# Queries and keys of one graph formed node by node and then transposed, the residual's transpose stored whole and split in the expert stage, in a fused graph-attention and mixture-of-experts kernel

## The reference

```python
# attention part, added to x
h = layernorm(x)
q, k, v = h @ Wq.T, h @ Wk.T, h @ Wv.T + bv            # in 12 heads of 32
a = einsum('bnhd,bmhd->bhnm', q, k) * SCALE + adj[:, None]
a = where(all(a == 0, axis=-1), -inf, a)
o = einsum('bhnm,bmhd->bnhd', nan_to_num(softmax(a)), v)
x = x + o @ Wo.T + bo
# expert part, added to x
u = layernorm(x)
logits = mean_over_nodes(u) @ router_w.T + router_b    # the two best experts of each graph
hid = act_e(u @ w1[e] + b1[e])                         # gelu, silu, mish, gelu
y = u + sum_e gate[e] * (hid @ w2[e] + b2[e])
out = x + layernorm(y) * ln_g + ln_b
```

## Time and profile before

| | |
|---|---|
| median of 3 runs | 1639.47 us (1636.82 to 1640.29) |
| the profiled execution, its own time | 1638.12 us |
| its span from first to last instruction | 1636.0 us |
| PE busy | 1590.5 us, 97% of the span |
| DVE busy | 1209.8 us, 74% |
| ACT busy | 955.6 us, 58% |
| POOL busy | 689.6 us, 42% |
| mean granted clock of TensorE | 0.993 of full speed |
| attention stage, first to last `scores` | 25.53 to 699.37 us |

### The profile page before, as it was taken

One profiled execution on the slowest core, in us unless ns is written; L12 is line 12 of the kernel. 1 busy time (PEld: TensorE's weight loads), 2 busy tenths in 40 slices (PEclk: granted clock), 3 DMA queues, 4 the chain that ended last, 5 costly groups with the idle time before them and its releaser, 6 DMA issues.

```text
span 1636.0 us, 46011 instructions
## 1 busy us (share of the span) xinstructions
PE 1590.5 (97%) x12720; PEld 1528.0 (93%) x12721; DVE 1209.8 (74%) x3750; ACT 955.6 (58%) x2819; POOL 689.6 (42%) x1106
## 2 busy tenths in 40 slices
PE   8999999999999999779999999999999999999998
PEld 7999999999999999769999999999999999999998
DVE  5788888888888888657766666676776767677766
ACT  6899999999999988753422232333334323243332
POOL 3787888878888777531111111111111111111112
PEclk9999999999999999889999999999999999999999
DMA  6444433455545543673222222222222222222211
GB/s 190 153 138 138 136 129 132 147 168 182 176 169 172 182 134 133 253 301 105 71 74 74 74 74 74 74 74 74 67 70 71 65 74 74 74 74 65 83 59 45
DMA packets 93804, 189.09 MB, mean 116 GB/s; under 512 B 10337, under 2 KB 57441, under 8 KB 92385
## 3 DMA queue, kind: packets, MB, share of 16 engines
q1 hardware_dynamic: 91664, 170.17, 31.6%
q10 hardware_dynamic: 1872, 15.73, 2.5%
HBM read 108.80 MB, written 77.07 MB: 114 GB/s over the span
## 4 chain that ended last, share of the span: by engine, by line
PE 89%; DVE 3%; issue 2%; ACT 2%; DMA 1%; POOL 1%; DVEq 1%; ACTq 0%; POOLq 0%; SPq 0%
PE bank L460 69%; PE bank L534 5%; PE bank L667 5%; PE bank L487 3%; PE bank L557 3%; PE bank L574 2%; PE bank L543 1%; PE bank L566 1%; DMA ut_scratch<-ut_out 1%; DVE half_t L1371 1%; DVE inverse L1378 1%; DVE inverse L1374 1%; ACT at_hi L944 0%; ACT inverse L951 0%; ACT prob L737 0%
## 5 line engine op out<-in xcount | busy, mean ns | idle before, releaser
L460 PE MATMUL bank<-w_hi,ut_in 128*128 x1536 | 423.7, 343 | 0.8 <-issue 0.4
L460 PE MATMUL bank<-w_both,at_hi 128*128 x1524 | 389.1, 336 | 7.4 <-DVE at_lo L1343 7.3
L737 ACT ACTIVATE prob<-att,heads 128x128 f32<-128x128 f32 x768 | 297.4, 390 | 14.2 <-DVE heads L1108 10.3
L460 PEld LDWEIGHTS bank<-w_both,at_hi 128*128 128x128 f32 x1524 | 274.3, 188 | 12.3 <-issue 12.2
L460 PEld LDWEIGHTS bank<-w_hi,ut_in 128*128 128x128 f32 x1536 | 281.5, 189 | 1.3 <-issue 1.3
L460 PE MATMUL bank<-w_lo,ut_in 128*128 x768 | 258.2, 336 | 0.0
L460 PE MATMUL bank<-w_both,at_lo 128*128 x762 | 255.3, 335 | 0.0
L875 ACT ACTIVATE hid<-hid 128x384 f32<-128x384 f32 x192 | 95.1, 526 | 270.5 <-DVE hid L1264 270.5
L944 ACT ACTIVATE at_hi<-bank,gate_col 128x384 fp32r<-128x384 f32 x254 | 133.4, 576 | 199.6 <-PE bank L667 197.8
L1264 DVE TENSOR_TENSOR hid<-bank,b_wide 128x384 f32<-128x384 f32 x256 | 130.9, 552 | 147.6 <-PE bank L460 138.9
L1072 POOL TENSOR_SCALAR rs_z<-mv_z 128x1 f32<-128x1 f32 x64 | 34.9, 545 | 433.1 <-DVE mv_z L1397 433.1
(11 more groups left out here) (139 smaller groups left out, 3475.7 us busy)
## 6 DMA issues: line engine op xcount, KB each, us to landing
xu_scratch<-xu SPq DMA_DIRECT2D x64, 384.0 KB, 2.3
ut_scratch<-ut_out SPq DMA_DIRECT2D x64, 384.0 KB, 2.7
ut_in<-ut_scratch SPq DMA_DIRECT2D x64, 384.0 KB, 3.0
xz<-xu_scratch SPq DMA_DIRECT2D x64, 384.0 KB, 3.2
x_in<-in_x SPq DMA_DIRECT2D x32, 384.0 KB, 4.7
xu<-in_x SPq DMA_DIRECT2D x32, 384.0 KB, 4.3
out_dram<-xz SPq DMA_DIRECT2D x64, 192.0 KB, 2.2
w_lo<-in_L_ffn_w SPq DMA_DIRECT2D x4, 1152.0 KB, 5.9
```

What stands on the lines that cost most here:

```text
L460: last = nc.tensor.matmul(acc, lhs[c][a], rhs[c][b], start=start and n == 0, stop=stop and n == len(terms) - 1)
L737: nc.scalar.activation(prob[g][:, hh, :], att[g][:, head, :], ACT.Exp, bias=neg_max[g][:, head:head + 1], scale=-1.0, accum_out=row_sum[g] ...
```

## The change

Queries and keys are now formed as values are: the transposed input of one graph is held still and the 384 columns of the weights stream past, which gives nodes on the partitions. Two products of 9 matmuls of 384 columns (`project_qk(h + 1)`) go into one double bank, `both`. DVE copies both to `qk_nat` in one instruction of 768 columns (`take_qk`), PE transposes them in six transposes (`transpose_qk`), and ACT copies and scales them into `q_t` and `k_t`. Each buffer now holds one graph, and the pipeline reaches less far ahead: `transpose_x` works on graph `h + 3` instead of `h + 5`, `project_v` on `h + 1` instead of `h + 2`, and the stage has two steps fewer ahead of step 0.

The transpose of `u` is stored once, unrounded (`take_u`), which removes `rest_of_u` on DVE; the expert stage splits it after it is loaded, with `round_ut` on ACT and `rest_of_ut` on DVE, and `first_layer` waits for the second of these.

On PE `project_v` now stands ahead of `spread_inverse`. On POOL `add_output_bias` works on graph `h - 2` instead of `h - 1` and stands ahead of `root2` instead of behind `fold_scores`. `load_residual` is issued at odd steps. Memory is laid out anew, and the loads of the experts' weights near the end of the stage start at other steps.

```diff
-        STEPS = range(-6, B + 4)
+        STEPS = range(-4, B + 4)
...
-                if h % 2 == 1 and 2 <= t + 4 < PAIRS:
-                    reached(sp, xn_done, 2 * (t + 2) + 2)
-                    load_x(t + 4)
+                if h % 2 == 1 and 2 <= t + 3 < PAIRS:
+                    reached(sp, xn_done, 2 * (t + 1) + 2)
+                    load_x(t + 3)
+                if h % 2 == 1 and 2 <= t < PAIRS:
+                    for g in range(2):
+                        sp.wait_ge(xu_stored[t % 2][g], 16 * (t // 2))
+                    load_residual(t)
...
+                reached(pe, qk_done, 2 * (n + 1))
...
-            def project_qk(h):
-
-                m, t = h % 2, pair(h + 2)
-                if h < 0:
-                    pe.wait_ge(wt_lo_done, (m + 1) * DC)
-                reached(pe, xt_lo_done, 2 * t + 2)
-                reached(pe, qk_done, qk_count(h - 1))
-                reached(pe, ot_done, h - 1)
-                reached(pe, inv_taken, h - 1)
-                for oc in range(DC):
-                    acc = bank[4 + oc // 2][:, (oc % 2) * 2 * N:(oc % 2 + 1) * 2 * N]
-                    last = split_product(acc, [(wt_hi[m][:, c, oc * P:(oc + 1) * P], wt_lo[m][:, c, oc * P:(oc + 1) * P]) for c in range(DC)],
-                                         [(xt_hi[t % 2][:, c, :], xt_lo[t % 2][:, c, :]) for c in range(DC)])
-                    if oc > 0:
-                        last.then_inc(qk_mm, 1)
+            def project_qk(n):
+
+                if n == 0:
+                    pe.wait_ge(wt_lo_done, 2 * DC)
+                reached(pe, xt_lo_done, n + 1)
+                reached(pe, ot_done, n - 2)
+                reached(pe, inv_taken, n - 2)
+                for m in range(2):
+                    last = split_product(both[:, m, 0:D], [(xt_hi[n % 2][:, c, :], xt_lo[n % 2][:, c, :]) for c in range(DC)],
+                                         [(wt_hi[m][:, c, :], wt_lo[m][:, c, :]) for c in range(DC)])
+                last.then_inc(qk_mm, 1)
+
+            def transpose_qk(n):
+                reached(pe, qk_taken, n + 1)
+                for m in range(2):
+                    for c in range(DC):
+                        last = nc.tensor.transpose(both[:, m, c * N:(c + 1) * N], qk_nat[:, m, c * P:(c + 1) * P], ident[:])
+                    last.then_inc(qkt_mm, 1)
...
+                reached(pe, ut_split, b + 1)
...
-                if has_qk(h):
-                    project_qk(h)
+                if has(h + 1):
+                    project_qk(h + 1)
+                if h == -1:
+                    transpose_weights(3)
...
+                if has(h + 1):
+                    transpose_qk(h + 1)
                 if has(h - 3):
                     transpose_u(h - 3)
                 if has(h - 1) and h != B:
                     transpose_probs(h - 1, 2)
+                if has(h + 1):
+                    project_v(h + 1)
                 if has(h - 1):
                     spread_inverse(h - 1)
-                if has(h + 2):
-                    project_v(h + 2)
                 if h == B - 11:
                     logits(0)
                 if has(h - 1):
                     attend(h - 1)
-                if has(h + 5):
-                    transpose_x(h + 5)
-                if h == -4:
-                    transpose_weights(1)
-                    transpose_weights(2)
-                if h == -2:
-                    transpose_weights(3)
+                if has(h + 3):
+                    transpose_x(h + 3)
+                if h in (-3, -2):
+                    transpose_weights(h + 4)
...
+            def take_qk(n):
+                reached(act, s_mm, n)
+                for m, (to, scale) in enumerate(((q_t, SCALE), (k_t, 1.0))):
+                    reached(act, qkt_mm, 2 * n + m + 1)
+                    nc.scalar.activation(flat(to[:]), both[:, m, 0:D], ACT.Copy, scale=scale).then_inc(qk_done, 1)
...
+            def take_u(n):
                 g = n % 2
                 reached(act, ut_mm, n + 1)
                 reached(act, ut_stored[g], 16 * (n // 2))
-                nc.scalar.activation(flat(ut_out[g][:, 0]), bank[3][:, 0:D], ACT.Copy).then_inc(ut_hi_done, 1)
+                nc.scalar.activation(flat(ut_out[g][:]), bank[3][:, 0:D], ACT.Copy).then_inc(ut_taken, 1)
...
+            def load_under_stages(h):
+                e = h - (FIRST + 2 * PIECES + 3)
+                if e == 0:
                     for p in range(3):
                         act.wait_ge(hi_stored[p], 16 * (2 * PIECES // 3))
                         act.wait_ge(lo_stored[p], 16 * (PIECES // 3))
-                    load_w1_hi(0)
-                if h == B - 4:
+                if 0 <= e < E - 1:
+                    load_w1_hi(e)
+                if h == B - 3:
                     act.wait_ge(xn_done, B)
-                    act.wait_ge(v_mm, B - 2)
-                    act.wait_ge(qk_mm, 2 * B - 2)
-                    act.dma_start(b1_wide[:].rearrange("p e s f -> p (e s f)"), b1.rearrange("(o e) f -> o (e f)", o=1).partition_broadcast(P)).then_inc(b1_loaded, 16)
-                    load_w1_hi(1)
-                if h == B - 3:
-                    act.wait_ge(qk_mm, 2 * B)
-                    load_w1_hi(2)
-                    act.wait_ge(s_mm, B - 2)
-                    load_w2("unused", "qk0")
-
-            def load_under_values():
+                    load_w1_hi(E - 1)
+
+            def load_under_projections():
                 act.wait_ge(v_mm, B)
-                load_w1_hi(3)
-                load_w2("xt1", "xt1")
+                load_w2("unused", "wv")
...
+            def round_ut(b, m, lap):
+
+                reached(act, ut_loaded[m % 2], 16 * (2 * lap + m // 2 + 1))
+                nc.scalar.activation(flat(ut_in[m % 2][:, 0]), flat(ut_in[m % 2][:, 1]).bitcast(F32), ACT.Copy).then_inc(ut_rounded, 1)
...
                 if has(h - 1):
                     take_probs(h - 1, 0)
                     take_probs(h - 1, 1)
+                if has(h + 1):
+                    take_qk(h + 1)
                 if h == B - 1:
                     load_under_scores()
-                if h == B:
-                    load_under_probs()
+                if h in (B - 1, B):
+                    load_under_probs(h - 1)
+                if h == B - 1:
+                    round_ut(0, 0, 0)
+                if h == B + 1:
+                    round_ut(1, 1, 0)
                 if has(h - 3):
-                    round_u(h - 3)
+                    take_u(h - 3)
                 if has(h - 1):
                     take_inverse(h - 1)
-                if has(h + 5):
-                    normalise_x(h + 5)
-                if h == -5:
+                if has(h + 3):
+                    normalise_x(h + 3)
...
+                if h == 2:
+                    pool.wait_ge(small_loaded, 16 * (2 + DC))
+                if has(h - 2):
+                    add_output_bias(h - 2)
                 if has(h - 3):
                     root2(h - 3)
                 if has(h):
                     fold_scores(h)
-                if h == 0:
-                    pool.wait_ge(small_loaded, 16 * (2 + DC))
-                if has(h - 1):
-                    add_output_bias(h - 1)
-                if has(h + 6):
-                    root1(h + 6)
+                if has(h + 4):
+                    root1(h + 4)
...
+            def take_qk(n):
+
+                reached(dve, qk_mm, n + 1)
+                reached(dve, qkt_mm, 2 * n)
+                nc.vector.tensor_copy(qk_nat[:], both[:, :, 0:D]).then_inc(qk_taken, 1)
...
-            def rest_of_u(n):
-                g = n % 2
-                reached(dve, ut_hi_done, n + 1)
-                nc.vector.tensor_tensor(flat(ut_out[g][:, 1]), bank[3][:, 0:D], flat(ut_out[g][:, 0]).bitcast(F32), ALU.subtract).then_inc(ut_lo_done, 1)
...
+            def rest_of_ut(b, m, lap):
+                reached(dve, ut_rounded, b + 1)
+                raw_half = flat(ut_in[m % 2][:, 1])
+                nc.vector.tensor_tensor(raw_half, raw_half.bitcast(F32), flat(ut_in[m % 2][:, 0]).bitcast(F32), ALU.subtract).then_inc(ut_split, 1)
...
+                if has(h + 1):
+                    take_qk(h + 1)
...
-                if has(h - 3):
-                    rest_of_u(h - 3)
-                if has(h + 6):
-                    input_stats(h + 6)
-                if h == -2:
+                if h in (B, B + 1):
+                    rest_of_ut(h - B, h - B, 0)
+                if has(h + 4):
+                    input_stats(h + 4)
...
+                if has(h + 1):
+                    take_v(h + 1)
...
+                    if k == 0 and graph(b, 1) and not (isinstance(b, int) and b < 1):
+                        rest_of_ut(b + 1, (m + 1) % 4, lap + (m + 1) // 4)```

The first place is on PE, in the second half of a step in the middle of the attention stage, from the transposes of the probabilities to the transpose of the next normalised input. Before:

```order
```

(31 more changed lines are left out.)

144 lines of the change are left out of this document (51 added, 93 removed).

## The result

The changed kernel takes **1697.8 us** (median of 4 runs, 1693.7 to 1698.9) against 1639.7 of the kernel before (1636.8 to 1640.3): the ratio is 1.035, 95% interval 1.033 to 1.038, so 58 us slower. The forecast was 1702, in a range of 1672 to 1718.

The account below looks back on a forecast made before the run. All four engines were read as close to full, PE busiest; two hand-over loops above PE's 11.25 us were to set a step of 11.78. Terms 59 + 1 + 3 = +63 us gave 1701, stated as 1702, range 1672 to 1718.

Parts of the forecast that it names:

- PE's own work, 11.25 us: Attention step on PE: 10.70 less 0.10 for the matmuls plus 0.65 for six new transposes gives 11.25 us.
- PE's work alone sets the step: Rival for the attention step: both loops shorter than read by 0.5 us, step 11.25, total 1670; chance 0.10.
- The first loop, 11.78: Attention step, take_inverse through POOL's bias and root, normalise_x1, transposes, values and inverse transposes: 11.78 us, setting the step.
- the 1.10 for the bias between guard and root: POOL in the attention step: output bias of 1.03 us and a gap add 1.10 us ahead of root2.
- The second loop, 11.72: Attention step, inverse's transposes, take_inverse, normalising and transposing the next input: 11.72 us, PE standing 0.45 us a step.
- DVE's copy at no cost: Attention step: the 768-column copy takes 0.95 us on DVE, ends before its transposes are due, costs PE nothing.
- The start: Ahead of first scores 2 to 3 us gained, 2 given back after: third scores at 40.8 instead of 41.82.
- The steps: Third to last scores: 61 steps of 11.78 us less 1.0, last scores at 758.4 against 699.37, +59.0 us.
- Behind the last scores: After the last scores: bias ahead of root2 costs 1 us once, expert-stage subtraction 3 us (bounds 0 and 8).
- The stall gone: End of attention stage: POOL's 9.57 us and PE's 8.55 vanish, the last xu load issued earlier, ahead of large weight loads.
- The sum: Whole kernel: 59 + 1 + 3 = +63 us, on the profiled 1638.12 giving 1701, stated as 1702.

Follow-up runs that it names:

- two kernels: Changed kernel with normalise_x ahead of take_inverse and four of six query/key transposes left out: 1658.6 us; the same with the output bias behind root2: 1639.3 us.
- the one on `xn`: Changed kernel with normalise_x(h + 3) moved ahead of take_inverse(h - 1) on ACT: 1669.1 us, ratio 1.018.
- the part alone: Kernel before with only u's transpose stored whole by ACT, then rounded and subtracted in the expert stage: 1639.8 us, ratio 1.000.
- The first experiment on it: Kernel before with only the output bias moved, for graph h - 2 ahead of root2 on POOL: 1638.7 us, ratio 0.999.
- the first experiment: Changed kernel with the output bias on POOL put back behind the folds, for graph h - 1: 1695.3 us, ratio 1.034.

## Why the prediction was right, and where its terms were off

- **PE's own work, 11.25 us.** Measured 11.24, with PE free of waits. The six transposes at 0.109 us were right (0.65 in the trace, 0.64 to 0.66 by doubling them). The 18 matmuls of queries and keys take 304.50 - 301.24 = 3.26 us where 3.23 was forecast and the 27 before took 3.33, and the values 1.66 (309.93 - 308.27) for 1.70. The rival "PE's work alone sets the step" gave 1670; the kernel in which it holds takes 1669.1.
- **The first loop, 11.78.** The loop exists, and two kernels show it by what the bias's place costs. Its size was over-read: `normalise_x1` starts 8.00 us after the last `take_inverse` (306.75 - 298.75, which is 310.45 less one step) and not 8.12. The term at fault is the 1.10 for the bias between guard and root. From its start to the root's it does take 1.10, but it starts 0.17 us after the start of the guard, where the root before started 0.29 us after it (311.96 - 311.67), so only 0.98 is added. With this and the values' 1.66 the loop is about 11.63. The trace agrees that it had slack: ACT ends `xu` at 307.46 and PE comes to it at 307.58, 0.12 us later, where a hand-over takes 0.05.
- **The second loop, 11.72.** Measured 11.70, and PE's stand 0.46 for 0.45. It set the step, by about 0.07 us over the other. So the mechanism was named (two closed loops above PE's work), but the wrong one of the two as the longer; that this cost so little is luck, since they happen to lie close together. The experiment on the bias and the one on `xn` tell them apart.
- **DVE's copy at no cost.** 0.95 us, as sized, over 1.28 us early; a wait for `qk_nat` shows only at the start (1.05 us ahead of 30.41), as said there.
- **The start.** Forecast: third scores at 40.8. Measured 43.30. I had counted 2 to 3 us won ahead of the first scores; it was 0.44. PE waits 1.24 us there for the split of the weights, and the eleven slow matmuls shown above cost about 1.7 us more than at the later pace, which the prediction did not have. This term was off by 2.5 us.
- **The steps.** 61 steps from the third to the last scores took 712.0 us, 11.67 each, against 717.6 in the forecast. With the late start the last scores came at 755.3 for 758.4.
- **Behind the last scores.** +2.6 us for +4. The bias ahead of the root, the expert stage's subtraction and the new order of the weight loads are in it, not told apart; the part alone shows the subtraction as 0.8 us of wait more than the earlier trace rows and nothing that the median can tell. By the Trainium skill's rule a DVE instruction with two SBUF inputs and a GpSimd one that reads SBUF shut each other out (SBUF — State Buffer, section SBUF: two separate sides). The changed kernel's subtractions last 0.545 to 0.561 us each, and no cost of such a lock shows on the path, which does not test the rule.
- **The stall gone.** Right, and for the reason given, the load's place. The first experiment on it tried the bias instead and missed. In the changed kernel the last load of `xu` is issued at 754.21, 0.95 us ahead of 3584 KB of weights (755.16), and a load of `ut_in` at 755.45 just behind them. The order was tested by experiment only on the kernel before, but the times to landing of these two (last column) fit it:

```profile
xu<-in_x SPq DMA_DIRECT2D x1, 384.0 KB, 4.8
...
ut_in<-ut_scratch SPq DMA_DIRECT2D x1, 192.0 KB, 14.3
```


The sum came to 1701 for the profiled execution; it took 1696.8. The 4 us are 5.6 of shorter steps and 1.4 behind them, less 2.5 of start; the rest is rounding in the terms. So the sum is closer than its terms, because the late start and the shorter steps cancel in part.

What stays open: why the first matmuls at the start ran at the slower pace, and whether 2.5 us for the bias in the first experiment is real behind the last scores, as it did not come again.

## What to carry to other kernels

When all engines are busy for three quarters of the time or more, write the step as closed loops of hand-overs, each from one use of a result to the same use a step later, and compare their lengths with the busiest engine's work; moving one instruction past a wait on the same engine (here two rows on ACT) was worth 29 us, half of the whole loss. Loops nest: a place that is worth 2 us under a longer loop is worth 19 when that is shortened, so an edit is priced only against what is next. And before moving the user of a late transfer, look at what was issued ahead of the transfer.

## What the runs showed of the hardware

A small load suffers from large ones issued just before it on another engine's queue, and by bytes more than an equal share would have it. In the kernel before, from 676 to 682.1 us (queue: packets, MB, share of the sixteen engines' time):

```profile
q10 hardware_dynamic: 219, 1.79, 77.6%
q1 hardware_dynamic: 165, 0.41, 16.8%
...
w_hi<-w1h_scratch ACTq DMA_DIRECT2D x1, 1152.0 KB, 5.7
xu<-in_x SPq DMA_DIRECT2D x1, 384.0 KB, 12.3
```

Here q10 is the queue of the large loads and q1 that of SP. In this window q10 moved 4.4 times the bytes of q1 (1.79 to 0.41 MB) but only 1.3 times the packets (219 to 165): its packets are 8.2 KB in the mean, the others' 2.5 KB. From 676 to 690 us of the kernel with the bias alone it is 5.2 times the bytes (4.50 to 0.87 MB) at 1.2 times the packets (506 to 436). Turns taken by packets would give such numbers; no run here changed the size of packets, so this is an inference. The 384 KB took 12.3 us to land. Issued at the same moment with the large loads a step later, the same load landed in 3.7 us:

```profile
xu<-in_x SPq DMA_DIRECT2D x1, 384.0 KB, 3.7
```
